# A three-part decoder layer: last chunk's maxima in another order, contexts copied behind the half copies, three openings reordered

## The reference

```python
x = x + retention(layernorm(x), Wq, bq, ..., gn_w, gn_b, decay)   # 16 heads of 16
x = x + cross(layernorm(x), ctx_512, Wq, w_kc_q, w_kc_kv, W_qr, W_kr, Wo)
x = x + ffn(layernorm(x), w1, w2, w3)

# retention: D[i, j] = exp(decay * (i - j)) where i >= j, else 0
ret = jnp.einsum('bhid,bhjd->bhij', q, k) * D[None]
ret = ret / clip(abs(ret.sum(-1)), 1.0, None);  attn = ret @ v
# group norm over each head, times silu(x @ Wg + bg), then @ Wo + bo
# cross: queries of 64 numbers for each head, rotated keys kv_r = rope(ctx_512)
scores = jnp.einsum('bhsr,bhlr->bhsl', q_r, k_r)
attn = softmax(scores, -1);  ctx_c = attn @ kv_r
ctx_lat = jnp.einsum('bhsd,hkd->bhsk', ctx_c, w_kc_kv);  out = ctx_lat @ Wo.T
# ffn: weights rounded to -1, 0, 1 by their mean magnitude
hidden = sigmoid(x @ q(w1).T) * (x @ q(w2).T);  out = hidden @ q(w3).T
```

## Time and profile before

| what | value |
|---|---|
| median of three runs | 2366.55 us (2366.11 to 2372.65) |
| profiled execution's own time | 2369.99 us |
| its span | 2368.2 us |
| TensorE busy | 2213.0 us, 93% |
| GpSimd busy | 1823.1 us, 77% |
| VectorE busy | 1682.3 us, 71% |
| ScalarE busy | 1194.9 us, 50% |

### The profile page before, as it was taken

The page is one execution under the profiler, slowest core; times in us unless marked ns, Lnnn a source line. Parts: engine busy times, 40 slices in busy tenths (PEclk is TensorE's granted clock), DMA queues, the critical chain, the costliest instruction groups (busy, mean ns, idle before and its releaser), DMA issues. The chain is left out here.

```text
span 2368.2 us, 47305 instructions
## 1 busy us (share of the span) xinstructions
PE 2213.0 (93%) x15390; PEld 1430.2 (60%) x15390; DVE 1682.3 (71%) x2774; ACT 1194.9 (50%) x1929; POOL 1823.1 (77%) x818
## 2 busy tenths in 40 slices
PE   6888947999997999999999999999999999999898
PEld 4565536777774555555555555555555555555588
DVE  5878747888875767767767767767767767767775
ACT  3332312223222566666666666666666666665243
POOL 2546434998995599999999999999999999998311
PEclk9989868999997899999999999999999999999899
DMA  5000013666667342432432432432432432431011
GB/s 142 21 17 25 14 50 104 190 186 181 191 188 204 73 108 66 98 96 65 98 96 65 98 96 65 98 96 65 98 96 65 98 96 65 98 90 39 18 49 42
DMA packets 239499, 216.07 MB, mean 91 GB/s; under 512 B 124500, under 2 KB 213768, under 8 KB 239304
## 3 DMA queue, kind: packets, MB, share of 16 engines
q1 hardware_dynamic: 239432, 215.22, 35.9%
HBM read 129.68 MB, written 60.78 MB: 80 GB/s over the span
## 5 line engine op out<-in xcount | busy, mean ns | idle before, releaser
L1741 POOL TENSOR_TENSOR x_acc<-x_acc,x_prob 128x1600 f32<-128x1600 f32 x315 | 1137.5, 3611 | 34.6 <-ACT x_prob L1769 13.1
L1769 ACT ACTIVATE x_prob<-x_scores 128x800 f32<-128x800 f32 (+1 forms) x768 | 602.1, 837 | 22.6 <-PE x_scores L2053 13.2
L2086 PE MATMUL x_context<-x_prob,x_kv 128*64 128x400 f32 x2816 | 551.2, 512 | 0.0
L1867 DVE TENSOR_REDUCE x_mx<-x_ring 115x2 f32<-115x1024 f32 x310 | 380.1, 1226 | 26.3 <-PE x_ring L2153 9.9
L1876 DVE TENSOR_REDUCE x_mx<-x_ring 115x1 f32<-115x466 f32 (+3 forms) x352 | 222.0, 631 | 234.3 <-PE x_ring L2160 233.8
L1789 ACT COPY x_half<-x_ring 115x466 f32<-115x466 f32 (+3 forms) x352 | 190.5, 541 | 338.6 <-PE x_ring L2160 338.6
L2086 PEld LDWEIGHTS x_context<-x_prob,x_kv 128*64 128x64 f32 x2816 | 171.0, 136 | 231.1 <-issue 225.5
L2053 PE MATMUL x_scores<-x_qh,x_dh 64*128 64x400 f32 (+1 forms) x1536 | 272.6, 349 | 0.0
L2053 PE MATMUL x_scores<-x_qh,x_dl 64*128 64x400 f32 (+1 forms) x1536 | 267.3, 342 | 0.0
L2053 PE MATMUL x_scores<-x_ql,x_dh 64*128 64x400 f32 (+1 forms) x1536 | 267.2, 342 | 0.0
L1880 DVE TENSOR_REDUCE x_mx<-x_half 115x1 f32<-115x466 f32 (+3 forms) x352 | 220.4, 626 | 24.4 <-ACT x_half L1789 22.4
(11 more groups left out here) (200 smaller groups left out, 3651.4 us busy)
## 6 DMA issues: line engine op xcount, KB each, us to landing
scratch_qh<-q_qsh SPq DMA_DIRECT2D x64, 200.0 KB, 3.2
scratch_ql<-q_qsl SPq DMA_DIRECT2D x64, 200.0 KB, 3.4
x_qm<-scratch_qh SPq DMA_DIRECT2D x64, 200.0 KB, 3.6
x_qh<-scratch_qh SPq DMA_DIRECT2D x64, 200.0 KB, 3.4
x_ql<-scratch_ql SPq DMA_DIRECT2D x64, 200.0 KB, 3.7
x_rden<-scratch_rden SPq DMA_DIRECT2D x64, 200.0 KB, 3.5
scratch_kr<-q_krot SPq DMA_DIRECT2D x32, 384.0 KB, 2.3
x_kr<-scratch_kr SPq DMA_DIRECT2D x32, 384.0 KB, 4.6
```

The costliest lines, as they stand in the source:

```text
L1741: pool.tensor_tensor(acc[0:rows, parity], first, prob[0:rows, c % PR], ALU.add).then_inc(acc_done.sem, 1)
L1769: act.activation(prob[0:rows, c % PR, u * HALF:(u + 1) * HALF].rearrange("p (j s) -> p j s", j=2), psc[0:rows, u, :, 0:BANK], ACT.Exp).the ...
L1867: dve.tensor_reduce(best[0:block_rows(r), :, r, i], src[0:block_rows(r), :, 0:b - a], AX.X, ALU.max).then_inc(read_sem(u), 1)
L2086: mm = pe.matmul(pav[DC * s:DC * s + DC, j, 0:BANK], kv[0:rows, parity, c], prob[0:rows, c % PR, cols], start=c == 0, stop=c == LC - 2)
```

## The change

It has four parts.

- *Retention opening.* ScalarE's 16 exponentials of the decay mask move behind the first copy of turned rows. On VectorE the statistics of group 1 and the mask's multiplication move behind both splits of weights.
- *Order of the last chunk.* In chunk 11 the wide maximum comes first and the half pair behind the scores. ScalarE copies the half block there between its two exponentials. The overall maxima wait for the half reads too.
- *Contexts.* `save_context` moves from the end of chunk 0 to chunk 1, behind that chunk's half copy.
- *Last batch and FFN opening.* The four normalising instructions on VectorE become four activations on ScalarE in chunk 5, with a shift that VectorE computes in chunk 3. The turn of the rows and their high copies move from chunk 6 to 8, the low parts from 7 to 9, `quantise(2)` from chunk 11 to 9, ahead of the late sums, of which one moves to chunk 10. Statistics and normalising of the FFN's second group move into the end of cross attention, ahead of and behind the last output's add.

```diff
--- before.py
+++ after.py
@@ -345,9 +345,6 @@
             for s in (act_read, av_copied):
                 act.sem_inc(s.sem, s.credit)
-            for h in range(H):
-                act.activation(dmask[:, h], rel[:], ACT.Exp, scale=decay[:, h:h + 1]).then_inc(decay_exp.sem, 1)
-
             def copy_xnT(k):
@@ -407,6 +404,8 @@
             copy_xnT(0)
+            for h in range(H):
+                act.activation(dmask[:, h], rel[:], ACT.Exp, scale=decay[:, h:h + 1]).then_inc(decay_exp.sem, 1)
             for w in range(2):
                 copy_qk(0, w)
@@ -566,18 +565,18 @@
             row_variances(0)
             normalise(0, 0, range(GB))
-            row_sums(1, 1, range(GB))
-            row_variances(1)
             dve.wait_ge(weights_loaded.sem, W_ALL)
             split_weights(wqk, wqkh, wqkl, 1)
             split_low(0)
+            dve.wait_ge(later_loaded.sem, LATER_ALL)
+            split_weights(wvg, wvgh, wvgl, 2)
+            row_sums(1, 1, range(GB))
+            row_variances(1)
             dve.wait_ge(decay_exp.sem, H)
             dve.tensor_tensor(dmask[:], dmask[:], causal[:].unsqueeze(1).broadcast_to([S, H, S]),
             dve.wait_ge(mask_ready.sem, 1)
             dve.wait_ge(constants.sem, 2)
-            dve.wait_ge(later_loaded.sem, LATER_ALL)
-            split_weights(wvg, wvgh, wvgl, 2)
             for b in range(GB):
                 read_vg(0, 0, b)
@@ -1471,14 +1470,16 @@
         for c in range(LC):
             own = []
-            if c > 0:
-                r, i = next(narrow)
-                own += [("half", r, i, 0), ("half", r, i, 1)]
+            r, i = next(narrow) if c > 0 else (None, None)
+            pair = [("half", r, i, 0), ("half", r, i, 1)] * (c > 0)
+            own += pair if c < LC - 1 else [next(wide)]
             own += [("scores", 0), ("scores", 1)]
             if c == 2:
                 own += [("den",), ("turn", 2)]
-            elif c > 0:
+            elif 0 < c < LC - 1:
                 own.append(next(wide))
+            elif c == LC - 1:
+                own += pair
             own.append(("context",))
             if c == LC - 1:
@@ -1747,6 +1748,8 @@
             in_turn(pool, slot)
+            pool.wait_ge(f.row_veps.sem, f.row_veps.at(1, 1))
+            pool.tensor_tensor(f.rstd[:], f.veps[:], f.mhalf[:], ALU.pow).then_inc(f.row_rstd.sem, 1)
         @block.scalar
@@ -1788,6 +1791,12 @@
                 act.copy(half[rows, k % 2, 0:b - a], ring[rows, rg.banks[u][0], 0:b - a]).then_inc(read_sem(u), 1)
+            def copy_halves(n, c):
+
+                for u in beside[c]:
+                    if u in copied and made_at(n, u):
+                        copy_half(n, u)
+
             def save_den(n):
@@ -1805,23 +1814,31 @@
                 for c in range(LC):
-                    for u in beside[c]:
-                        if u in copied and made_at(n, u):
-                            copy_half(n, u)
+                    if c < LC - 1:
+                        copy_halves(n, c)
+                    if c == 1 and not is_at(n, -1) and not is_at(n, 0):
+                        save_context(n)
                     if is_at(n, -1) and 3 <= c < 3 + H // 2:
                         act.wait_ge(wco_filled.sem, c - 2)
                     if not is_at(n, -1):
                         for u in range(2):
+                            if c == LC - 1 and u == 1:
+                                copy_halves(n, c)
                             exponentials(n, c, u)
-                        if c == 0 and not is_at(n, 0):
-                            save_context(n)
+                    elif c == LC - 1:
+                        copy_halves(n, c)
                     for u in beside[c]:
                         if u[0] == "den":
                         elif u[0] == "turn" and made_at(n, u):
                             copy_turn(n, parity if u[1] < 2 else 1 - parity, u[1])
-                    if is_at(n, B - 1) and c == 6:
+                    if is_at(n, B - 1) and c == 5:
+                        act.wait_ge(f.row_steps.sem, 2)
+                        for b in range(GB):
+                            act.activation(f.xn[:, b], f.x[:, 0, b], ACT.Identity, scale=f.rstd[:, b:b + 1],
+                                           bias=f.shift[:, b:b + 1]).then_inc(f.xn_ready.sem, 1)
+                    if is_at(n, B - 1) and c == 8:
                         for i in range(EC):
                             act.wait_ge(f.xn_turned.sem, f.xn_turned.at(0, i + 1))
@@ -1887,8 +1904,8 @@
             def slot(n, parity):
                 for c in range(LC):
-                    if is_at(n, B - 1) and c == LC - 1:
-                        for k in range(1, 4):
+                    if is_at(n, B - 1) and c >= LC - 2:
+                        for k in (1,) if c == LC - 2 else (2, 3):
                             late_sum(k, 8 + k)
                     for u in beside[c]:
@@ -1903,6 +1920,8 @@
                         elif u[0] == "mT":
                             wait_read(dve, n, last_max)
+                            wait_read(dve, n, (*copied[-1][:3], 0))
+                            dve.wait_ge(half_read.sem, half_read.at(n, len(copied)))
                             dve.tensor_reduce(negm[:], mx[:], AX.X, ALU.max, negate=True).then_inc(max_ready.sem, 1)
                             turn_maxima(n)
@@ -1950,16 +1969,33 @@
                     dve.bn_stats(f.stats[:, b], f.x[:, 0, b]).then_inc(f.row_stats.sem, 1)
                 dve.wait_ge(f.row_stats.sem, f.row_stats.at(0, GB))
-                dve.sem_inc(f.stats_complete.sem, 1)
+                dve.sem_inc(f.row_steps.sem, 1)
                 for b in range(GB):
                     dve.bn_aggr(f.mv[:, b], f.stats[:, b]).then_inc(f.row_mv.sem, 1)
                 dve.tensor_scalar(f.veps[:], f.mv[:, :, 1], EPS, None, ALU.add).then_inc(f.row_veps.sem, 1)
-            def normalise_rows():
+            def shift_rows():
                 dve.wait_ge(f.row_rstd.sem, f.row_rstd.at(0, 1))
+                dve.scalar_tensor_tensor(f.shift[:], f.mv[:, :, 0], -1.0, f.rstd[:], ALU.mult,
+                                         ALU.mult).then_inc(f.row_steps.sem, 1)
+
+            def second_rows():
+                dve.wait_ge(f.x_loaded.sems[1], f.x_loaded.done(1, 1))
                 for b in range(GB):
-                    dve.tensor_scalar(f.xn[:, b], f.x[:, 0, b], f.mv[:, b, 0:1], f.rstd[:, b:b + 1],
+                    dve.bn_stats(f.stats[:, b], f.x[:, 1, b]).then_inc(f.row_stats.sem, 1)
+                dve.wait_ge(f.row_stats.sem, f.row_stats.at(1, GB))
+                dve.sem_inc(f.row_steps.sem, 1)
+                for b in range(GB):
+                    dve.bn_aggr(f.mv[:, b], f.stats[:, b]).then_inc(f.row_mv.sem, 1)
+                dve.wait_ge(f.row_mv.sem, f.row_mv.at(1, GB))
+                dve.tensor_scalar(f.veps[:], f.mv[:, :, 1], EPS, None, ALU.add).then_inc(f.row_veps.sem, 1)
+
+            def normalise_second():
+                dve.wait_ge(f.row_rstd.sem, f.row_rstd.at(1, 1))
+                dve.wait_ge(f.xn_turned.sem, f.xn_turned.at(0, EC))
+                for b in range(GB):
+                    dve.tensor_scalar(f.xn[:, b], f.x[:, 1, b], f.mv[:, b, 0:1], f.rstd[:, b:b + 1],
                                       ALU.subtract, ALU.mult).then_inc(f.xn_ready.sem, 1)
@@ -1985,16 +2021,17 @@
                 elif c == 1:
                     first_rows()
+                elif c == 3:
+                    shift_rows()
                 elif c == 4:
-                    normalise_rows()
                     thresholds()
                     quantise(0)
                     late_sum(0, 6)
                 elif c == 7:
+                    quantise(1)
+                elif c == 9:
                     split_rows()
-                    quantise(1)
-                elif c == LC - 1:
                     quantise(2)
@@ -2017,7 +2054,9 @@
             for j in range(2):
                 last_context(j)
+            second_rows()
             output(B + 1, 1)
+            normalise_second()
         @block.tensor
@@ -2373,7 +2413,7 @@
             def slot(k, parity, more):
-                if more:
+                if more and not is_first(k):
                     rows_rstd(k + 1)
...
@@ -2467,9 +2507,9 @@
                     if m >= 1:
                         low(k, parity, m - 1)
-                    if m == 0 and more:
+                    if m == 0 and more and not is_first(k):
                         row_statistics(k + 1, 1 - parity)
-                    if m == 2 and more:
+                    if m == 2 and more and not is_first(k):
                         normalise(k + 1, 1 - parity)
                     if m >= 2 and not is_first(k):
```

7 lines of the change are left out of this document (4 added, 3 removed).

## The result

The changed kernel is slower by 0.3%: 2373.35 us median against 2366.33 for the kernel before in the same sessions (18 runs each), a ratio of 1.0032 with a 95% interval of 1.0021 to 1.0042, which is 5 to 10 us. One of the 18 runs of before took 3559.67 us; it is left out of the ratio, and the two medians differ by some 7 us with it or without. The forecast was 2361.2 us and its range ended at 2367. The profiled execution of the changed kernel took 2366.92 us and is the fastest of its 18, while that of before took 2369.99, more than 14 of the 18 runs of before; so the two traces show where each part went, but their spans mustn't be subtracted.

What follows compares the result with a forecast made beforehand. TensorE sets the pace, the loop bound by it with VectorE's last reads, GpSimd close behind. Retention -9.3, loop +6.0, last batch +1.0, FFN -3.0 sum to -5.3 from 2366.55: 2361.2 us; 8-in-10 range 2347 to 2367.

Steps and rivals of the forecast that it cites:

- The last chunk: Cross loop, chunk 11: half blocks behind the scores leave VectorE's reads uncovered, a cost of 0.6 us a batch on the path.
- H: Chunk 11's first block start, 1313.54 before; after, half blocks at H+1.8, overall maximum at H+3.7 instead of H+3.12.
- The first chunks: Cross loop, chunks 0 and 1: maximum no longer waits, contexts start at 1325.94 instead of 1326.35, gain 0.4 us a batch.
- the loop's sum: Cross loop: +0.18 us a batch for 30 batches and +0.6 in batch 0, together +6 us, bounds -11 to +8.
- rival 3: Loop: the context copy holds back chunk 0's contexts until 1326.35 or later, no 0.4 gain; 2373.8 us, chance 0.06.
- Retention: Retention's opening: first projection at 13.2, scores of group 0 near 27, -9.3 us (-8 to -10).
- The last batch: Last cross batch: quantising waits for GpSimd's sums, totals start at 2211.5, reciprocal at 2212.9; +1.0 us (-3.9 to +1.7).
- rival 2: Last batch: VectorE and GpSimd run side by side, or second chain shorter; -3.9 instead of +1.0, 2356.3 us, chance 0.1.
- The FFN's opening: FFN start: group 1 already normalised, so TensorE doesn't wait 2.42 us; -3.0 us (-2.4 to -4.3).
- Rival 1: Cross loop: GpSimd sets it, last chunk's 0.6 is free, gain 0 to 0.3 a batch; about 2350 us, chance 0.25.

Runs made afterwards that it cites:

- the run with the old tail and the three other parts: Kernel before with the new retention opening, last chunk's order and moved context copy, but old last batch and FFN opening: 2372.37 us, 1.0028 of before.

## Why the prediction was wrong

**The last chunk**, 0.6 us a batch: right on the path, down to the half blocks at H+1.8 and the overall maximum at H+3.7; undone, it gives 17.6 us back. TensorE's idle time was 0.24 and not 0.4, since the forecast took the start of the next matmul for the end of the scores, which the path doesn't depend on.

**The first chunks**, 0.4 us a batch: this term failed. The forecast had the copy end at 1325.88 and the contexts 0.06 later. The copy's end was as forecast (9.26 behind the overall maximum, forecast 9.22), but TensorE started 0.24 behind it. The 0.06 is about the step of the wait that the change takes away: there the half copy ended at 1325.88 and TensorE started at 1325.93. The forecast took that step over to another wait, where it is four times as long. So the gain was 0.23, and 0.17 times 30 batches is 5 us. Why one step is 0.05 and the other 0.24 is not shown.

**What the loop's sum left out**: the pass ahead of batch 0 makes maxima too and is 0.8 us longer (from the last query product to the first overall maximum 45.7 us against 44.9), and batch 1 is 1.3 longer than the loop's change explains. With these two the loop cost 13 us in the traces, where +6 were forecast. The bounds, -11 to +8, were too narrow on that side: they held no case in which the gain fell short while the cost stood. That case was rival 3, at 0.06, with the whole gain gone; half of it came. Its 2373.8 us lies beside the measured 2373.35 by luck: the contexts started at 9.50 behind the overall maximum and not at the old 9.69 or later, as it asked.

**Retention**, -9.3: right within what the runs can tell, -8.5 (5 to 12 us less) by the opening alone, and by undoing it -8.6 by medians or -4.3 by ratios. In the traces the first projection came 8.2 earlier and the scores 8.9. Within it the first projection came 1.2 late, since the exponentials had hidden the load of ScalarE's table.

**The last batch**, +1.0: the totals started 50.0 us behind the last overall maximum, forecast 50.5, so the sums on VectorE and GpSimd were right, and rival 2 wrong: beside GpSimd's sum the subtraction of the second quantising took 4.28 us (the row at 2194.03) where the first had taken 0.95. That a GpSimd instruction and a VectorE instruction with two SBUF inputs or in a two-port mode exclude each other is what the Trainium skill says (SBUF — State Buffer, Who interferes with whom). The trace agrees: the subtraction of 0.95 us ended 0.8 us behind GpSimd's sum, which ran until 2197.55. The reciprocal came at 53.0 and not 51.9: it stood 2.98 us behind the start of the totals, where the forecast took half of 2.91. Behind a gap of 4.15 us, where the forecast had about 2, the totals ran at a granted clock of 0.50, and the forecast had kept their price at the full clock.

**The FFN's opening**, -3.0: it gave 4.0 in the two traces, and 5.1 between the means of the ten kernels with it (136.6) and the four without (141.7), more than the bound of 4.3. The granted clock at the FFN's start could be the cause. It is read over 20 us that begin 1 to 2 us behind the first product. These rows are of the opening alone, of the changed kernel, and of the run with the old tail and the three other parts:

```profile
2218.00:2238.00 20.00, 16.38 (x77) 15.01 (x76) 12.59 (x31) 8.04 (x17) 2.89 (x2) 0.82 0.07 22
...
2227.00:2247.00 20.00, 18.38 (x105) 17.26 (x103) 13.14 (x31) 9.57 (x21) 2.87 (x2) 0.93 0.08 22
...
2225.00:2245.00 20.00, 15.34 (x87) 14.00 (x86) 13.88 (x38) 8.01 (x17) 3.05 (x3) 0.96 0.08 22
```

0.82 and 0.93 would be a tenth of 20 us, 2 us. But the third has 0.96 with the old opening, and its FFN took 142.2 us, longer than the 141.9 of the first. So the clock doesn't account for the gain, and why it is 4 to 5 us and not 3 stays open.

**Rival 1**, that GpSimd sets the loop, at 0.25: not in this kernel; it does from 44.12 us down, 0.3 us below the old batch. The distance that the forecast read, 0.15 us, was about half of that, but the right sign, since the first 0.3 us that other engines gave up brought GpSimd to the front.

**What is not explained.** The forecast missed by 12 us. The loop accounts for 7 of them (13 in place of 6), while the other terms came out 2 to 3 below the forecast in the traces. The rest is open: the parts' traces, added up with the mean start of the queries, give some 7 us less than the medians show (-10 for retention, +13 for the loop, +1 and -5 for the tail). Runs that undo one part each give +5.8 by medians and +14.1 by ratios, and their own intervals reach 3 to 5 us to either side. The delay in batch 1 with the new tail has a place but no cause.

The best kernel of the study has the change without its new last chunk, with the context copy in two and the third quantising where it was: 2349.33 us, 0.9927 of before. Its interval overlaps with those of the three other kernels that have two context copies and the old last chunk and were run as often (0.9931 to 0.9934).

## What to carry to other kernels

Before a unit with many readers is put last in a chunk, look at what covers its reads: here the scores covered two reads of 0.69 us for nothing, and taking that cover away cost 0.58 us in each batch. When a wait is moved from one place to another, don't take over the step from the releasing engine's end to the start of the next: it was 0.05 us at the old wait and 0.24 at the new one. Let the sum of a loop include the passes written out ahead of it. Where a plan makes a gap on TensorE like the 4.15 us here, cost the next matmuls at the lower clock too.

## What the runs showed of the hardware

A context matmul started 0.24 us behind the end of the ScalarE copy that it waited for, and a matmul of the maxima 0.05 us behind the end of its copy. TensorE's granted clock was 0.50 in 16 matmuls behind an idle stretch of 4.15 us (5.60 us for them), and 1.00 behind one of 1.37 (2.91 us), in two kernels that differ only in where the third quantising stands. In two other traces with the same 4.15 us the 16 took 4.60. ScalarE's table load took 1.28 us at 11.36 as at 8.45, and costs time on the path only where nothing hides it. The granted clock over 320 us of retention was 0.86 and 0.84 in two executions with the same instructions there, which went with 7 us of time.
